# A decoder layer on one core: convolution over 36 instead of 40 product columns, wrap copies four heads at a time, a split last store, and new instruction orders on all engines

## The reference

```python
x = x + attn(layernorm(x), Wq, Wk, Wv, Wo)     # 16 heads of 16; scores * tril mask, softmax(scores / sqrt(T)), values, Wo
x = x + xattn(ctx, ctx, layernorm(x), ssm_kernel, D, 8)
x = x + ffn(layernorm(x), gate, up, down)      # 256 -> 2048 -> 256, 4-bit codes with scales, gelu(gate) * up
```

```python
kv  = einsum('bhil,bhjl->bijhl', k, v)                      # products of two channels of one head
y   = irfft(rfft(kv) * rfft(ssm_kernel))[..., :L]           # causal convolution along l
out = y + kv * D
out = einsum('bijhl,bhil->bjhl', out, q)
```

## Time and profile before

| | us |
|---|---|
| median of 3 runs | 250.36 |
| the profiled execution | 251.04 |
| its span, first to last instruction | 249.3 |
| PE busy | 228.1 (91%) |
| DVE busy | 163.0 (65%) |
| POOL busy | 147.4 (59%) |
| ACT busy | 133.7 (54%) |
| granted TensorE clock | 1.000 of 2.4 GHz throughout |

### The profile page before, as it was taken

The page is one execution under the profiler, slowest core; times in us unless marked ns, Lnnn a source line. Parts: engine busy times, 40 slices in busy tenths (PEclk is TensorE's granted clock), DMA queues, the critical chain, the costliest instruction groups (busy, mean ns, idle before and its releaser), DMA issues.

```text
span 249.3 us, 5605 instructions
## 1 busy us (share of the span) xinstructions
PE 228.1 (91%) x2148; PEld 144.3 (58%) x2148; DVE 163.0 (65%) x290; ACT 133.7 (54%) x289; POOL 147.4 (59%) x174
## 2 busy tenths in 40 slices
PE   7799997997796979986999999999999999999992
PEld 7574774554463546653447586565665656556562
DVE  3889899996969899996769964236262362412134
ACT  2447898897584689655854443253152531523320
POOL 4169898592428999978997613461735617323130
PEclk9999999999999999999999999999999999999999
DMA  6985999367132102200120000021030000000005
GB/s 174 339 236 157 170 231 307 82 145 176 47 126 76 59 4 77 56 3 0 48 78 4 0 0 3 0 71 58 0 129 3 0 0 3 0 0 0 3 1 168
DMA packets 15059, 18.90 MB, mean 76 GB/s; under 512 B 1368, under 2 KB 12728, under 8 KB 15032
## 3 DMA queue, kind: packets, MB, share of 16 engines
q1 hardware_dynamic: 15032, 18.53, 26.8%
HBM read 15.23 MB, written 3.17 MB: 74 GB/s over the span
## 4 chain that ended last, share of the span: by engine, by line
PE 64%; DVE 10%; POOL 6%; ACT 5%; DMA 5%; issue 4%; SPq 4%; DVEq 0%; ACTq 0%
PE bank L1357 37%; PE bank L1538 16%; DMA X<-in_x 3%; POOL arena L482 3%; DVE mx L1047 2%; DMA XN<-in_down_scale 2%; DVE kvp L1022 2%; PE bank L1609 2%; DVE arena L1029 2%; POOL arena L485 2%; SPq L317 1%; POOL w L498 1%; PE bank L1607 1%; ACT PT L671 1%; ACT arena L637 1%
## 5 line engine op out<-in xcount | busy, mean ns | idle before, releaser
L506 POOL TENSOR_TENSOR QK<-QK 128x512 f16<-128x512 f32 x24 | 27.8, 1158 | 56.4 <-ACT QK L700 56.4
L1123 DVE SCALAR_TENSOR_TENSOR QK<-bank,QK 128x512 f32<-128x512 f32 x32 | 22.0, 689 | 59.0 <-PE bank L1357 59.0
L710 ACT ACTIVATE QK<-bank 128x512 f32<-128x512 f32 x32 | 18.9, 595 | 59.7 <-PE bank L1357 59.4
L1357 PE MATMUL bank<-xTh,Wa 128*128 128x512 f16 x128 | 40.5, 379 | 0.7 <-DVE xTl L1148 0.7
L1357 PE MATMUL bank<-xTh,Wb 128*128 128x512 f16 x128 | 40.5, 379 | 0.0
L482 POOL TENSOR_TENSOR arena<-Ys,qx 128x640 f32<-128x640 f32 x16 | 27.4, 1715 | 5.9 <-ACT qx L753 5.7
L1357 PE MATMUL bank<-xTl,Wb 128*128 128x512 f16 x64 | 24.3, 379 | 0.0
L1357 PE MATMUL bank<-xTl,Wa 128*128 128x512 f16 x64 | 24.3, 379 | 0.0
L1538 PE MATMUL bank<-Wa,QK 128*128 128x256 f16 x192 | 23.4, 273 | 0.0
L1538 PE MATMUL bank<-Wb,QK 128*128 128x256 f16 x192 | 23.3, 273 | 0.0
L1538 PEld LDWEIGHTS bank<-Wa,QK 128*128 128x128 f16 x192 | 18.8, 98 | 4.7
(11 more groups left out here) (132 smaller groups left out, 472.6 us busy)
## 6 DMA issues: line engine op xcount, KB each, us to landing
arena<-in_codes SPq DMA_DIRECT2D x6, 384.0 KB
arena<-kscr SPq DMA_DIRECT2D x2, 1024.0 KB, 7.7
QK<-qk_scratch SPq DMA_DIRECT2D x8, 256.0 KB, 5.0
arena<-in_ctx SPq DMA_DIRECT2D x2, 768.0 KB, 6.9
qk_scratch<-Wa SPq DMA_DIRECT2D x12, 128.0 KB, 3.6
arena<-in_gu_scale SPq DMA_DIRECT2D x6, 256.0 KB
QK<-qk_scratch SPq DMA_DIRECT2D x8, 128.0 KB, 5.1
out<-XN SPq DMA_DIRECT2D x4, 256.0 KB, 2.4
```

Source lines behind the costliest of these rows:

```text
L506: g_.tensor_tensor(il[:, u % IR], val[:, u % VR], ih[:, u % IR], ALU.subtract).then_inc(s_il, 1)
L710: s_.activation(val[:, u % VR], bank[2 * (u % 2)][:, :], ACT.Gelu_apprx_tanh, scale=1.0 / W_GAIN).then_inc(s_gel, 1)
L1123: v_.scalar_tensor_tensor(out=val[:, u % VR], in0=bank[2 * (u % 2) + 1][:, :], scalar=UP_SCALE, in1=val[:, u % VR], op0=ALU.mult, op1=ALU. ...
L1357: ins = mmul(out, a(c), w(c), start=(n == 0), stop=(n == 3 * len(chunks) - 1))
```

## The change

1. `convolve` reads 36 of each batch's 40 columns and writes 36 of 40 (8 x 36 = 288 columns), for all 144 matmuls.
2. The second copy of `conv_out` (the wrap: 72 elements per partition, 32 of them) is dropped. `wrap_round(g)` takes its place: two copies inside Ys for each group of four heads, one that fills the four repeated columns (256 elements) and one for the wrap (576 elements), 8 instructions in all.
3. The last two batches are stored singly: batch 6 by SP, batch 7 from ACT's queue.
4. The call lists of SP, POOL, ACT, DVE and PE are ordered anew. The idle matmuls keep their number and write to other columns of two banks in turn.

```diff
+NUNIQ = 36
...
             load_skip()
+            load_x(2, 2)
             load_w(0)
+            load_ctx(0)
             load_w(1)
             load_w(2)
-            load_x(2, 2)
-            load_ctx(0)
+            load_ctx(1)
             store_taps()
-            load_ctx(1)
+            fill_minus()
             load_toeplitz(0)
-            fill_minus()
+            early_codes(0)
             store_qk(0, 0, 0)
...
-            load_wo()
+            early_codes(2)
             max_rows(3)
-            early_codes(2)
+            early_codes(3)
             max_rows(4)
-            early_codes(3)
...
-            for b in range(0, B, 2):
-                sp.wait_ge(s_fin, b + 2)
-                sp.dma_start(out_d[b:b + 2].rearrange("b t d -> t b d"), XN[:, b:b + 2, :]).then_inc(s_out, 16)
-            sp.wait_ge(s_out, 16 * B // 2)
+            for b, n in ((0, 2), (2, 2), (4, 2), (6, 1)):
+                sp.wait_ge(s_fin, b + n)
+                sp.dma_start(out_d[b:b + n].rearrange("b t d -> t b d"), XN[:, b:b + n, :]).then_inc(s_out, 16)
+            sp.wait_ge(s_out, 16 * 5)
...
-                s_.activation(view(Ys[:, h, lc], [[YROW, B], [DIAG, 3], [1, 3]], HD),
-                              view(conv_bank(h, lc)[:, 0:320], [[40, B], [HD, 3], [1, 3]], HD + 5),
-                              ACT.Copy).then_inc(s_ys[lc], 1)
+            def wrap_round(g):
+
+                for lc in range(2):
+                    sc.wait_ge(s_ys[lc], 4 * g + 4)
+                rows = Ys[:, 4 * g, 0]
+                every = [YROW, 4 * 2 * B]
+                s_.activation(view(rows, [every, [1, 4]], 4 * DIAG + 4), view(rows, [every, [1, 4]], 4 * DIAG),
+                              ACT.Copy).then_inc(s_wrap, 1)
+                s_.activation(view(rows, [every, [DIAG, 3], [1, 3]], HD),
+                              view(rows, [every, [DIAG, 3], [1, 3]], DIAG + 5), ACT.Copy).then_inc(s_wrap, 1)
...
+            sc.wait_ge(s_fin, B)
+            sc.dma_start(out_d[B - 1], XN[:, B - 1, :]).then_inc(s_out, 16)
...
             stats_x(2)
-            stats_x(3)
             apply_x(0)
             apply_x(1)
             split_taps()
+            stats_x(3)
+            stats_x(4)
+            stats_x(5)
+            stats_x(6)
             apply_x(2)
             apply_x(3)
+            stats_x(7)
+            x_lo(0)
             weight_lo(0)
...
-                for _ in range(n):
-                    mmul(bank[7][:, 0:P], ident[:, :], ident[:, :], start=True, stop=True)
+                for i in range(n):
+                    mmul(bank[6 + i % 2][:, 256:256 + P], ident[:, :], ident[:, :], start=True, stop=True)
...
-                out = conv_bank(h, lc)[:, 0:320]
+                out = view(conv_bank(h, lc)[:, 0:320], [[40, B], [1, NUNIQ]])
```

More of the change, by code:

```diff
@@ L538, in _ @@
             kv_lo(10)
+            max_pieces(0)
             products(12)
-            max_pieces(0)
             kv_lo(11)
+            kv_lo(12)
             products(13)
@@ L544, in _ @@
             decode_scale(0, 0)
-            kv_lo(12)
+            products(14)
             kv_lo(13)
-            products(14)
             products(15)
```

362 lines of the change are left out of this document (182 added, 180 removed).

## The result

The change takes 255.57 us in the median of its four executions beside 251.31 in four of the kernel before on the same chip. The ratio of the two, with the slow executions (over 1.5% above a kernel's fastest) left out, is 1.0152, with a 95% interval from 1.0079 to 1.0225: slower by about 1.5%. I had forecast 247.8 with a range up to 252.5; the time lies outside. The profiled execution took 255.49 us with a span of 253.8 (before: 251.04 and 249.3), and TensorE's mean granted clock in it was 0.977 instead of 1.000.

The account below looks back on a forecast made before the run. Feed-forward keeps PE full, so the end follows `gate_and_up(0)`; before it nearly full DVE and waits in the chain of batches 5 to 7 bound. +0.4 - 1.5 - 0.9 - 0.6 - 0.1 = -2.7, giving 247.8 us, range 245.0 to 252.5.

Parts of the forecast that it names:

- Start, +0.4: Start through batch 4's scores: later first product slips the convolution stage, mostly swallowed by DVE's wait; +0.4 us, bounds 0 and +2.
- at a granted clock of 1.00: Start: PE's first product expected near 12 us with TensorE still at its full 2.4 GHz.
- the rival of 0.14: Start: late start costs more, PE's pauses halve its clock during queries and keys; 254.2 us, chance 0.14.
- my 7.8 less 1.25: Late-start rival: 7.8 us run at half clock, less 1.25 swallowed by idle time before 60.28, +6.5 us.
- 1.0 less what a wait swallows: Convolution stage: slip of +1.0 us, of which DVE's wait for batch 4's scores swallows up to 1.25; +0.4 left.
- Codes of step 2, -1.5: DVE's 1.68 us wait to 73.58: codes issued 3.7 us earlier, so the wait goes; -1.5 us, bounds -1.7 and 0.
- both `probs`, -1.5: Attention of batches 5 and 7: `probs` put ahead of calls that wait for other engines; -0.9 and -0.6 us.
- The first rival: DVE's nearly full list: removed waits reappear at the next instruction, 0 to half the gains stay; 249.9 us, chance 0.28.
- 36 columns and wraps, 0: Convolution stage: savings on PE and ACT bring 0, since DVE sets the pace; at best -1.9 and -1 us.
- my 1.11: ACT's wrap copies: each of four rounds estimated at 0.42 and 0.69 us, 4 x 1.11 = 4.4 us added.
- End, -0.1: Last stores: half-size last store issued beside SP's, same bytes through full DMA engines; -0.1 us, 0 to -0.5.
- the feed-forward list, 0: Feed-forward stretch: its new call list counted at nothing, because PE has 12 matmuls of a unit queued; 0.

Follow-up runs that it names:

- e4: The change with more idle multiplications at the start (WARM 13, 11, 6 instead of 13, 2, 1): 253.51 us, ratio 1.0075.
- e1: The kernel before with the change's edits (36 columns, wrap rounds, split last store) but all five call lists as before: 251.13 us, ratio 1.0006.
- e6: e1 with the change's lists up to the end of the query and key projections, the new start alone: 253.16 us, ratio 1.0064.
- e11: The change with one swap on VectorE, `sum_slots(3,1)` ahead of `w_lo(2)`: 253.22 us, ratio 1.0102.
- e9: The change run again with no edit and more executions: 255.69 us, ratio 1.0177.
- e5: e4 with the old order of ScalarE and TensorE calls around `turn_query(0)`: 254.6 us, ratio 1.01.
- e7: e1 with one swap in SP's list, `early_codes(2)` before `max_rows(3)`: 251.46 us, ratio 1.0029.
- e3: The edits with the lists of before until about 60 us and the change's new lists behind that: 252.25 us, ratio 1.0024.
- e8: e1 with 40 columns again in every convolution instead of 36: 251.94 us, ratio 1.0025.
- e13: The change with both e4's idle multiplications at the start and e11's swap: 251.95 us, ratio 1.0032.
- e2: The change with the lists of before up to the end of the query and key projections on all engines: 253.71 us, ratio 1.0065.
- e12: e7 with a few idle multiplications in TensorE's pauses, at the start and at four later places: 252.81 us, ratio 1.0025.
- e10: The change with idle multiplications in TensorE's long pauses, at the start and at three later places, no order changed: 254.76 us, ratio 1.0135.
- e17: e15 with `pair_max(6,0)` ahead of `w_lo(1)` on VectorE: 257.05 us, ratio 1.0236.
- e15: e3 with e11's swap and e5's old order around `turn_query(0)`: 250.87 us, ratio 0.9982.
- e18: e15 run once more, with before on the same chip: 251.37 us, ratio 0.999.

## Why the prediction was wrong

- **Start, +0.4: the order was right, the clock was not.** The instructions came where I had put them (`x_lo(0)` 10.91, product 12.32, convolution 27.96 for 27.7). What failed is the step "at a granted clock of 1.00". I had this as the rival of 0.14, and took it as decisive for a large slip only. The runs put its price at 2.26 us at 60 in the profiled execution, with 6.6 us at half clock (10.2 to 16.8), not my 7.8 less 1.25. My chance was far too low: the earlier trace rows had pauses up to 1.4 us without a fall, and I made a pause of 2 us a mishap. That e4 has the +0.4 to the tenth is luck: it is -0.45 for the edits (e1), +0.79 for the new start at full clock (e6 against e1) and +0.06 for the rest, where I had 1.0 less what a wait swallows. Nothing was swallowed at 60 either: DVE's wait there grew from 1.25 to 1.79. On TensorE's clock the Trainium skill's page "TensorE: Matmul & The Clock Gate", section "Part 1: The HAM clock gate", says that idleness halves it and that the point at which it rises varies from run to run. The trace agrees on the first, with 0.50 behind 2.14 us of pause in the change; but 2.39 us had no fall in e6, and 2.20 none in the change.
- **The collision: not in my sum at all.** I had seen DVE and POOL slow each other and used it for the cadence of `products` only, not where a 0.27 us instruction stands on the path. It costs 2.56 us (e11 against e9). About 1.6 of it is the held shift (e5 against e1, at full clock), and the rest goes with the fall of the clock behind it. The Trainium skill's page "SBUF — State Buffer", section "Who interferes with whom", has it that a VectorE instruction with two inputs in that memory contends with a GpSimd one that reads it, and that the lock is exclusive. By that rule the shift ends with `w_lo(2)`, and a reduction with one input holds nobody: 110.33 and 110.27 in the change, 0.27 beside `sum_slots` in e11. The trace agrees on both. Which of two is held should go by the order of issue, and there the records do not agree: the held shift starts 0.03 us ahead of `w_lo(2)`.
- **Codes of step 2, -1.5: an earlier issue was taken for an earlier landing.** In the change the issue hardly moved, 67.62 for 67.90 and not 64.24, since `max_rows(2)` itself came at 66.08 instead of 62.84. Where it did move, VectorE waited until 72.86 all the same in e7, and found them there at 71.73 in e3.
- **These codes and both `probs`, -1.5: the waits went and nothing was gained.** The first rival, "the waits only change their names", holds for these terms. In the change the lag fell by 1.7 us up to 74.55 (74.55 - 73.58 = 0.97 against 66.91 - 64.19 = 2.72), as forecast, and was 1.6 again at pair 7's maxima. `probs(5,1)` came at 94.08, only 0.24 behind before, while `ln_apply(2,0)` behind it came 3.7 later (97.02 for 93.33). e3 has 1.34 us of gain at pair 6 and 0.28 at `w_lo(2)`, e7 has none.
- **36 columns and wraps, 0: right.** Triples 0.37 to 0.38 us, wraps 4 rounds of 0.42 + 0.83 us for my 1.11; e1 1.0006, e8 within 0.3%. The 0.9 us of e1's profiled execution is not resolved by its ratio.
- **End, -0.1, and the feed-forward list, 0: right.** The end takes 5.7 us before and after, and the span grew by no more than `gate_and_up(0)` slipped.

Put together from profiled executions, by the start of `gate_and_up(0)`: before 117.69, e1 116.78, e13 116.82, the change 122.15. So the edits bring 0.9, and the new orders with both repairs are level with e1. The 5.33 us between e13 and the change are 2.99 up to the last shift (105.50 against 108.49), where the two differ by the idle multiplications of the start alone, and 2.34 behind it, the collision and its fall. These are single executions; in the medians the two causes are worth 3.6 us.

The v projections inside the convolution stage are in none of these terms: in e2, with the old start, pair 0's first maxima are 2.1 us behind e1's and batch 4's 1.46; in e4 the same lists have 60.68. By e13 nothing of that survives to the end, but it was not tried apart.

What stays open: whether e5's order costs anything over e4's (its median is 1.1 higher, its profiled execution 2.0 faster), why the transfer of the codes was slow in e7, and whether e12's collision is in most of its executions; each has one trace.

## What to carry to other kernels

Before an order is changed, list TensorE's pauses it makes, not only the sum of waits: a pause of 2 us costs itself and often the half clock behind it (all ten executions of the change and 11 of 12 of e6 lost the clock somewhere). Idle multiplications cost nothing where they stand inside the pause (e4); where they wait for the same bank as the work behind them they come after it, and in e10 they cost 1.1 us. Where a short GpSimd instruction is a link of the chain, look at what VectorE runs at that moment; a swap of one call (e11) was worth 2.5 us in the median and the same sort of swap (e17) cost 5.7, so move a long call only into a stretch where its engine waits anyhow. And compare executions by their granted clock: the three of before that I predicted against had a median of 250.36, all 140 have 251.99. And a transfer that is issued earlier need not land earlier (e7): read the landing, not the issue.

## What the runs showed of the hardware

- A GpSimd scalar instruction of 0.27 us was held to 1.84, 1.86, 1.89 and 2.14 us beside a 1.75 us operation of VectorE on two tiles, each time to within 0.1 us of its end, and not at all beside a reduction of one tile (e11). At `w_lo(2)` the held ones started 0.03 us ahead of it to 0.02 behind, and those that started 0.26 us or more ahead were over in time.
- The same kernel loses the clock at different places: the repetition of the change (e9) at 11, 62 and 113 us, the first profiled execution at 10 and 112. Pauses of 1.80 and 1.81 us at the same instruction had a fall in one execution and none in the other, and the longest pause of the change, 2.20 us, had none.
- A fall does not need a long pause: e8 lost the clock at 81 and 94 with no single pause of 1 us; in the stretches just before, 79 to 80 and 94 to 95, TensorE was busy for 0.20 and 0.17 of 1 us.
- With idle multiplications the mean clock was 0.994 (e10), 0.997 (e12) and 0.994 (e13) against the change's 0.978; e15 and e18 have 0.994 without any added.
